# Part of the second layer's sums moved among the tiles of the fourth group, parked in DRAM and added back at the end

## The reference, cut to what matters

```python
h = relu(layernorm(x))
e = leaky_relu((h @ W @ a1)[:, None] + (V @ W @ a2)[None, :])     # V: entity_embs
att = softmax(where(adj > 0, e, -9e15), axis=1)
x1 = x + elu(att @ V + h)
h2 = relu(layernorm(x1))
agg = adj.T @ h2                       # sums over all rows j of adj[j, i] * h2[j]
out = x1 + relu(agg @ U.T / adj.sum(axis=0)[:, None])
```

## Time and profile before

| | |
|---|---|
| median of 3 runs | 389.12 us (388.97 to 389.73) |
| profiled execution, its own time | 388.29 us |
| its span, first to last instruction | 386.5 us |
| mean granted TensorE clock | 0.96 of 2.4 GHz |
| PE busy | 298.7 us (77%), 7586 matmuls |
| DVE busy | 297.3 us (77%) |
| ACT busy | 255.9 us (66%) |
| POOL busy | 114.0 us (29%) |
| HBM read, written | 72.76 MB, 2.11 MB |

### The profile page before, as it was taken

How to read it: one execution, slowest core, us unless ns; L and a number is a source line. 1 busy time by engine, 2 the same in 40 slices (tenths; PEclk the granted TensorE clock), 3 DMA queues, 4 the chain that set the end, 5 groups by cost and what they waited for, 6 DMA issues and landing times.

```text
span 386.5 us, 16271 instructions
## 1 busy us (share of the span) xinstructions
PE 298.7 (77%) x7586; PEld 276.0 (71%) x7586; DVE 297.3 (77%) x403; ACT 255.9 (66%) x316; POOL 114.0 (29%) x120
## 2 busy tenths in 40 slices
PE   1817666556777867578797878778899999999996
PEld 0712555556667756567687877678899999999996
DVE  8899989795998769699985998998988774008333
ACT  2312699689989897779989999996887781010000
POOL 8766287386140482030006111012111103010000
PEclk9956699799989999999999999999999999999999
DMA  8999999999999999995000001001110005102100
GB/s 163 136 109 109 106 109 108 138 109 107 111 123 124 102 109 106 103 104 92 3 4 3 3 4 57 2 3 33 30 30 5 3 5 103 35 2 45 32 22 19
DMA packets 26809, 25.24 MB, mean 65 GB/s; under 512 B 22041, under 2 KB 22105, under 8 KB 26742
## 3 DMA queue, kind: packets, MB, share of 16 engines
q0 software_dynamic: 4752, 16.90, 42.1%
q1 hardware_dynamic: 19830, 6.75, 7.8%
q10 hardware_dynamic: 2160, 0.56, 0.7%
HBM read 72.76 MB, written 2.11 MB: 194 GB/s over the span
## 4 chain that ended last, share of the span: by engine, by line
PE 30%; DVE 29%; ACT 16%; issue 9%; POOL 9%; DMA 6%; SPq 1%; POOLq 0%; DVEq 0%
DVE scratch L832 18%; PE q L1239 10%; PE w L1178 8%; ACT q L686 7%; PE w L1239 6%; DVE arena L884 6%; PE q L1153 5%; ACT arena L668 5%; ACT arena L672 3%; DMA adj_sb<-in_adj_dram 2%; POOL adj_sb L413 2%; DMA v_sb<-n_L_gnn_entity_embs_dram 2%; DMA bi<-rows_sb 2%; POOL stat_c L458 1%; POOL adj_sb L417 1%
## 5 line engine op out<-in xcount | busy, mean ns | idle before, releaser
L1178 PE MATMUL w<-v_sb,arena 128*64 128x65 f32 (+1 forms) x4224 | 155.7, 224 | 9.9 <-issue 8.3
L832 DVE CUSTOM_DVE_ANT_0 scratch<-adj_sb,t_row 125x2048 uint8<-125x2048 uint8 x66 | 153.2, 2322 | 1.6 <-DMA adj_sb<-in_adj_dram 0.3
L1178 PEld LDWEIGHTS w<-v_sb,arena 128*64 128x64 f32 (+1 forms) x4224 | 140.9, 138 | 11.6 <-issue 9.0
L1153 PE MATMUL q<-bi,adj_sb 128*64 128x125 bf16 x2112 | 93.9, 224 | 49.0 <-ACT q L686 41.9
L1153 PEld LDWEIGHTS q<-bi,adj_sb 128*64 128x64 fp8e4 x2112 | 70.4, 112 | 63.4 <-ACT q L686 51.6
L668 ACT ACTIVATE arena<-q,t_col 128x1000 f32<-128x1000 f32 (+2 forms) x102 | 88.5, 872 | 5.9 <-PE q L1153 5.7
L672 ACT ACTIVATE arena<-arena,t 128x1000 f32<-128x1000 f32 (+2 forms) x58 | 63.3, 1093 | 20.6 <-DVE arena L884 19.8
L884 DVE SCALAR_TENSOR_TENSOR arena<-arena,b_col,q 128x1000 f32<-128x1000 f32 (+1 forms) x43 | 52.3, 1224 | 17.4 <-PE q L1153 12.5
L686 ACT ACTIVATE q<-second_row,minus_b 128x750 f32<-128x750 f32 (+1 forms) x49 | 48.1, 981 | 1.3
L686 ACT ACTIVATE q<-arena,minus_b 128x375 f32<-128x375 f32 (+1 forms) x53 | 42.3, 799 | 1.3
L1239 PE MATMUL q<-g_all,adj_sb 124*128 124x129 f16 (+1 forms) x660 | 39.1, 220 | 0.0
(11 more groups left out here) (139 smaller groups left out, 203.6 us busy)
## 6 DMA issues: line engine op xcount, KB each, us to landing
adj_sb<-in_adj_dram POOLq DMA_DIRECT2D x33, 500.0 KB, 36.9
arena<-s_dram SPq DMA_DIRECT2D x2, 500.0 KB, 7.0
out_dram<-v_sb SPq DMA_DIRECT2D x10, 96.0 KB, 1.8
x_sb<-in_x_dram SPq DMA_DIRECT2D x1, 928.0 KB
v_sb<-x_dram SPq DMA_DIRECT2D x1, 768.0 KB, 5.3
v_sb<-n_L_gnn_entity_embs_dram ACTq DMA_DIRECT2D x2, 256.0 KB, 5.4
v_sb<-n_L_gnn_entity_embs_dram SPq DMA_DIRECT2D x2, 256.0 KB, 6.2
second_row<-s_dram SPq DMA_DIRECT2D x1, 500.0 KB, 3.7
```

What stands on the lines that cost most here:

```text
L832: nc.vector.tensor_tensor_reduce(out=junk[0:R, :], in0=adj_bytes[0:R, b, half], in1=t_row[0:R, half], scale=1.0 / ONE, scalar=0.0, op0=ALU ...
L1153: last = nc.tensor.matmul(q[n % Q_SLOTS][e:e + width, bank, start:start + R], weights, bi[:, i % BI_SLOTS, k, :], start=not ON_ACT[n] and ...
L1178: last = nc.tensor.matmul(att(i)[e0:e1, bank, place_in, :], e[:, k * R + e0:k * R + e1], v_sb[:, c, :], start=(c == 0 and place_in == 0), ...
```

## The change

Of the second layer's sums, those over blocks 0 to 8 for outputs 4 to 10 (chunks 12 to 31, 20 of the 32) are made behind tiles of the fourth group, one chunk of nine matmuls at a time, two chunks behind tiles 4, 13 and 28. They are collected in the first bank of `w`, three chunks at a time. ScalarE copies each finished bank into `stage`, which lies in the part of `x_sb` that held x1 of the first blocks, SP writes it to DRAM, and ScalarE's next copy waits until that has landed. At the end of the tile stages SP loads all of it into `t_row`. For outputs 4 to 10 `gather` starts at block 9, and VectorE adds the saved part first. To free `stage`, x1 of the first two groups is stored earlier in SP's queue; to free the bank, `turn_h2` of the third group writes the other one and waits for `s_copied`. The hand-written tables are new throughout. In the core of the diff below the new tables of the groups other than the fourth are cut.

```diff
-                 (1, 4, 6, 8, 10, 12, 28, 29, 30, 31),
-                 (0, 1, 2, 3, 4, 5, 6, 7, 9, 10, 11, ...
+                 (1, 3, 5, 7, 8, 10, 12, 28, 29, 30, 31),
+                 (0, 1, 2, 3, 4, 5, 6, 7, 8, 10, 11, ...
...
-                   (4, 9, 10, 12, 13, 16, 17, 17, 17, 19, 21, 21, 21, 21, 22, 23)]
+                   (4, 10, 13, 13, 13, 13, 16, 17, 17, 18, 20, 20, 21, 23, 23, 24)]
...
-        'elu_below': (None, 6, 7, 6, 8),
+        'elu_below': (None, 7, 7, 5, 8),
-        'scale': (None, 17, 14, 14, 16),
+        'scale': (None, 17, 14, 13, 16),
-        'times_u': (None, 22, 19, 23, 20),
+        'times_u': (None, 21, 19, 25, 21),
-        'copy_s': (15, 7, 18, 12, None),
+        'copy_s': (15, 9, 18, 12, None),
...
+    AHEAD = (4, 5, 6, 7, 8, 9, 10)
+    AHEAD_IN, AHEAD_BLOCKS = 3, 9
+    AHEAD_TILES = (3, 4, 4, 7, 8, 10, 12, 13, 13, 15, 16, 17, 19, 20, 21, 23, 24, 26, 28, 28)
+    AHEAD_COPIES = (5, 10, 13, 17, 22, 26, 30)
+    SAVES = (2, 4, 1)
...
         def turned_at(i):
-            return w[:, i % 2 * 2, :]
+            return w[:, i % 2 * 2 + (i == AHEAD_IN - 1), :]
...
             for i in range(1, NI):
+                if 2 <= i < NI - 1:
+                    sp.wait_ge(mean2_done, i - 1)
+                    store_x1(*GROUPS[i - 2])
+                if i == AHEAD_IN + 1:
+                    save(0, SAVES[0])
                 sp.wait_ge(s_copied, i)
...
+                if i == AHEAD_IN + 1:
+                    save(SAVES[0], SAVES[1])
                 sp.wait_ge(halves_copied, i)
...
-            for i in range(NI - 1):
+            save(SAVES[0] + SAVES[1], SAVES[2])
+            sp.wait_ge(part_saved, 16 * len(AHEAD))
+            sp.wait_ge(r1_ready, NI)
+            sp.dma_start(saved, saved_dram).then_inc(part_loaded, 16)
+            for i in range(2, NI - 1):
...
+            def save(first, n):
+                for k in range(first, first + n):
+                    c0, c1 = OUTS[AHEAD[k]]
+                    sp.wait_ge(part_copied, k + 1)
+                    first = k * 3 * (2 * D + 1)
+                    sp.dma_start(saved_dram[:, first:first + (c1 - c0) * (2 * D + 1)], stage[...]).then_inc(part_saved, 16)
...
+            def copy_ahead(k):
+                c0, c1 = OUTS[AHEAD[k]]
+                act.wait_ge(part_summed, k + 1)
+                if k == 0:
+                    act.wait_ge(x1_stored, 32)
+                    act.wait_ge(cen2_done, 2)
+                else:
+                    act.wait_ge(part_saved, 16 * k)
+                nc.scalar.activation(stage[...], ahead_bank()[...], ACT.Copy).then_inc(part_copied, 1)
...
+                if o in AHEAD:
+                    if o == AHEAD[0]:
+                        dve.wait_ge(part_loaded, 16)
+                    nc.vector.tensor_tensor(saved_sums(o), fresh_sums(o), saved_sums(o), ALU.add).then_inc(part_added, 1)
+                    dve.wait_ge(part_added, AHEAD.index(o) + 1)
...
+                if c == 0 and i == AHEAD_IN + 1:
+                    pe.wait_ge(part_copied, len(AHEAD))
...
+                if i == AHEAD_IN - 1:
+                    pe.wait_ge(s_copied, i + 2)
...
+            def sum_ahead(k, c):
+                c0, c1 = OUTS[AHEAD[k]]
+                if c == c0:
+                    if k == 0:
+                        pe.wait_ge(hp_done, AHEAD_IN)
+                        pe.wait_ge(lo_done, AHEAD_IN - 1)
+                        pe.wait_ge(ones_made, 1)
+                    else:
+                        pe.wait_ge(part_copied, k)
+                for b in range(AHEAD_BLOCKS):
+                    rows = rows_of(b)
+                    last = nc.tensor.matmul(ahead_bank()[:, ...], adj_sb[0:rows, b, c * P:(c + 1) * P], h2[0:rows, b, 0:2 * D + 1],
+                                            start=(b == 0 and c == c0), stop=(b == AHEAD_BLOCKS - 1 and c == c1 - 1))
+                if c == c1 - 1:
+                    last.then_inc(part_summed, 1)
...
+                if i == AHEAD_IN:
+                    for tile, chunk in zip(AHEAD_TILES, chunks_ahead):
+                        if tile == c:
+                            sum_ahead(*chunk)
...
             for o in (0, 1, 2, 3):
-                gather(o, 0, late)
+                gather(o, blocks_ahead(o), late)
             turn_h2(NI - 1)
-            gather(4, 0, late)
+            gather(4, blocks_ahead(4), late)
             times_u(NI - 1)
-            gather(5, 0, late)
+            gather(5, blocks_ahead(5), late)
...
-                gather(o, 0, NB)
+                gather(o, blocks_ahead(o), NB)
```

More of the change, by code:

```diff
@@ L180, in graph_layers_kernel @@
         junk = scratch[:, 0:512].bitcast(uint8)
+        saved = t_row[:, 0:sum(OUTS[o][1] - OUTS[o][0] for o in AHEAD) * (2 * D + 1)]
+        stage = x_sb[:, :, :].rearrange("p b d -> p (b d)")[:, 0:3 * (2 * D + 1)]
+        saved_dram = nc.dram_tensor("saved_dram", (P, sum(OUTS[o][1] - OUTS[o][0] for o in AHEAD) * (2 * D + 1)), fp32, kind="Internal").ap()
         s_dram = nc.dram_tensor("s_dram", (NI, 8 * R), fp32, kind="Internal").ap()
@@ L337, in out_bank, with ahead_bank, fresh_sums, saved_sums @@
             return banks[(0, 1, 2, 3, 4, 5, 6, 7)[o % 8]]
+        def ahead_bank():
+            return w[:, (AHEAD_IN - 1) % 2 * 2, :]
+        def fresh_sums(o):
+            c0, c1 = OUTS[o]
+            return out_bank(o)[:, 0:(c1 - c0) * (2 * D + 1)]
         def sums(o):
+            return (saved_sums(o) if o in AHEAD else fresh_sums(o)).rearrange("p (k d) -> p k d", d=2 * D + 1)
+        def saved_sums(o):
             c0, c1 = OUTS[o]
-            return out_bank(o)[:, 0:(c1 - c0) * (2 * D + 1)].rearrange("p (k d) -> p k d", d=2 * D + 1)
+            first = AHEAD.index(o) * 3 * (2 * D + 1)
+            return saved[:, first:first + (c1 - c0) * (2 * D + 1)]
+        def blocks_ahead(o):
+            return AHEAD_BLOCKS if o in AHEAD else 0
         @block.sync
@@ L355, in _, with store_x1 @@
                 sp.dma_start(u_sb[:, h * D:(h + 1) * D], U[:, :]).then_inc(u_in, 16)
+            def save(first, n):
[3 more added lines that the diff above has]
+                    first = k * 3 * (2 * D + 1)
+                    sp.dma_start(saved_dram[:, first:first + (c1 - c0) * (2 * D + 1)], stage[:, 0:(c1 - c0) * (2 * D + 1)]).then_inc(part_saved, 16)
+            def store_x1(b0, b1):
+                rows = rows_of(b0)
+                to = x1_dram[first_row(b0):first_row(b0) + (b1 - b0) * rows, :].rearrange("(k p) d -> p k d", p=rows)
+                sp.dma_start(to, x_sb[0:rows, b0:b1, :]).then_inc(x1_stored, 16)
             for i in range(1, NI):
@@ L718, in _ @@
                         copy_halves(i + 1)
+                if i == AHEAD_IN:
+                    for k, tile in enumerate(AHEAD_COPIES):
+                        if tile == c:
+                            copy_ahead(k)
                 if n + 2 < len(TILES) and ON_ACT[n + 2]:
@@ L1206, in times_u @@
                 last.then_inc(h2_multiplied, 1)
+            chunks_ahead = [(k, c) for k, o in enumerate(AHEAD) for c in range(*OUTS[o])]
+            def sum_ahead(k, c):
[9 more added lines that the diff above has]
+                    rows = rows_of(b)
+                    last = nc.tensor.matmul(ahead_bank()[:, (c - c0) * (2 * D + 1):(c - c0 + 1) * (2 * D + 1)],
+                                            adj_sb[0:rows, b, c * P:(c + 1) * P], h2[0:rows, b, 0:2 * D + 1],
+                                            start=(b == 0 and c == c0), stop=(b == AHEAD_BLOCKS - 1 and c == c1 - 1))
+                if c == c1 - 1:
+                    last.then_inc(part_summed, 1)
             rows()
@@ L1240, in gather @@
                                                 adj_sb[0:rows, b, c * P:(c + 1) * P], h2[0:rows, b, 0:2 * D + 1],
-                                                start=(b == 0 and c == c0), stop=(b == NB - 1 and c == c1 - 1))
+                                                start=(b == blocks_ahead(o) and c == c0), stop=(b == NB - 1 and c == c1 - 1))
                 if last_one == NB:
```

54 lines of the change are left out of this document (27 added, 27 removed), and 10 rows, old and new, of tables (DVE_TILES, GUARD_TILES).

## The result

The changed kernel takes 413.09 us (median of 4 runs, 412.55 to 414.33) against 389.29 us; the ratio is 1.0615, with a 95% interval of 1.0587 to 1.0643. It was forecast at 380.3 us and is 23.8 us slower instead of 8.8 faster. The profiled execution took 413.43 us, with a span of 411.6. Runs over 1.5% above the fastest of the same kernel are left out as slow, which in this document concerns only two of the six of `after_split`.

What follows compares the result with a forecast made beforehand. The prediction took TensorE to bound the end and VectorE to close the fourth group. Its terms, -10.5 + 0.4 + 1.3 = -8.8 us, took the median of 389.12 to 380.3 us, own range 379.2 to 382.3, wider range 378.6 to 384.8.

Steps and rivals of the forecast that it cites:

- the price of group 0's early store: SP's queue ahead of the third group: 12.8 us pass, row still in time, costed at nothing, at most some 8 us.
- Rival 2: Early x1 store holds the third group's row, which starts 7 us late: up to 387.5 us, half of that 384; chance 0.13.
- The end, -10.5 + 0.4: At the end, 180 matmuls removed save 10.5 us; only VectorE's last addition is on the path, costing 0.4 us.
- the cover: Output 5's early part, 48 matmuls or 2.8 us, still covers the last group's closing by 0.2 us; costed at nothing.
- The fourth group, +1.3: VectorE ends the fourth group later: 0.5 us at tile 12, 2.33 more for a guard, 1.5 less for a wait.
- rival 4: In the fourth group, ScalarE's copies wait for saves to land; kernel would take 395 us, slower; chance 0.04.
- rival 3: TensorE becomes the fourth group's bound, half of the 10.5 us landing on the path: 384.3 us; chance 0.10.
- The tables, 0 with 1 us to both sides: The other groups' new tables move steps by a tile or two, no direction seen: 0, 1 us either way.
- Rival 5: Change doesn't do what it says: gain void if the wait for the saved part held VectorE at output 4; chance 0.01.

Runs made afterwards that it cites:

- after_split: Changed kernel with each early x1 store cut in two, rows 0 to 111 and then 112 to 123; 379.83 us, ratio 0.978 to the kernel before.
- late_x1: Changed kernel with x1 of groups 0 and 1 stored behind the adjacency load, in SP's fourth round; 379.01 us, ratio 0.9733 to the kernel before.
- act_queue_group0: Changed kernel with group 0's early x1 store issued from ScalarE's queue instead of SP's, group 1's staying on SP; 377.90 us, one run.

## Why the prediction was wrong

The sign was wrong by one step: the price of group 0's early store. I wrote "Group 0's x1 is 372 rows of 256 bytes, 23 for an engine" and from it 12.8 us, a row that lands at 133 for a need at 134.28, and a cost of nothing. The price of a row, one adjacency packet of 0.55 us, was right (0.57 measured). So was the mechanism, a row that waits behind the store in SP's queue. The number of rows an engine was not: 93, not 23, as the store goes over four engines. With 93 the same sum gives 109.81 + 93 x 0.55 + 10.6 = 171.6 for the row's landing; ScalarE's relu came at 171.51. I took the sixteen engines for granted; no row shown before the run said how a store of 124 rows is spread, and I should have bounded it.

The Trainium skill has the rule (DMA: Bandwidth & Descriptors, section Why a DMA increments its semaphore by 16 and not by 1, on how many engines): a transfer goes over the largest number of engines up to 16 that divides the slowest dimension on both sides. By it 124 rows get four engines and 112 get sixteen, and the runs agree: 23.2 us for 124 rows, 18.4 for 336, with 4 and 16 packets left over. The profile doesn't number the engines, so which four they were is not shown.

Rival 2 named the place and the mechanism and had 0.13. Its price, 21 us for the store and up to 387.5, stopped short by the same error. Its lean on the arbitration of the Trainium skill (DMA: Bandwidth & Descriptors, section Queues, rings and completion order: a whole packet of 9 to 17 descriptors from one queue before the next) is not borne out here, as the profile counts packets: single rows alternate with single packets of 4 KB, 0.63 us apart. Its 0.9 us a packet was too high as well; rival 2 had the price of a row too large and the number of rows too small.

The other terms:
- **The end, -10.5 + 0.4.** Measured -10.1 (66.7 to 56.6), in every kernel with these 20 chunks ahead. In late_x1 the early part of outputs 4 and 5 and the work around it are:
```profile
338.22 2.96 PE L1335 MATMUL w<-g_all,adj_sb 124*128 124x129 f16 x48
341.02 1.09 PE L1277 MATMUL w<-uu,buf_b 128*125 128x128 f32 x8
341.94 2.96 PE L1335 MATMUL w<-g_all,adj_sb 124*128 124x129 f16 x48
344.75 5.76 PE L1335 MATMUL q<-g_all,adj_sb 124*128 124x129 f16 x96
```
  48 matmuls are 2.81 us from start to start, 58.5 ns each. POOL ends the low part at 343.40 + 1.12 = 344.52, and TensorE goes on at 344.75: the cover holds by the 0.2 us of the forecast:
```profile
343.40 1.12 POOL L569 TENSOR_TENSOR g_all<-buf_a,g_all 125x512 f16<-125x512 f32 x1 [13.51 <-ACT buf_a L709]
```
  The last addition is one of 0.43 us:
```profile
372.99 0.43 DVE L1085 TENSOR_TENSOR t_row<-q,t_row 128x258 f32<-128x258 f32 x1 [0.40 <-PE q L1335]
```
  The 81 ns a pair of the Trainium skill (TensorE: Matmul & The Clock Gate, section Back-to-back issue gap) would have taken 14.6 us from the end; the traces show 58.4 to 58.5 ns and 10.1 us, so here the measurement decides.
- **The fourth group, +1.3.** From its first mask to that of the fifth I had forecast 64.6 us; in the kernel after it is 236.80 to 301.19, 64.4. VectorE's last shift instruction came 59.5 us after the first mask, forecast 59.7. The lines of the kernel after, PE first:
```profile
236.80 0.65 PE L1220 MATMUL q<-bi,adj_sb 128*64 128x125 bf16 x16 [1.31 <-DMA bi<-rows_sb]
...
301.19 0.67 PE L1220 MATMUL q<-bi,adj_sb 128*64 128x125 bf16 x16
```
```profile
296.31 0.17 DVE L938 TENSOR_TENSOR halves<-neg_t,halves 125x8 bf16<-125x8 f32 x1
```
  The growth came with the new tables, in which the forecast had put it (the order of the guards), and not with the sums: with the new tables alone the same distance is 64.7 us, against 63.3 before. ScalarE's copies took 0.48 us (forecast 0.45), and the saves landed in 1.9 us, so rival 4 is out. TensorE's waits for ScalarE's relu in late_x1 fell to 1.6 us from the 12.2 of the earlier trace rows: the sums went where the idle time was. VectorE's scores waited 5.6 us for TensorE there, against 5.3 before, so rival 3 is out as well.
- **The tables, 0 with 1 us to both sides.** Measured -2 us (387.12 against 389.18), outside what I gave them. Without the early store the terms would have summed to -10.1 + 0.8 + 0.3 for the sums and -2 for the tables, -11.0; late_x1 shows -10.2. The 0.8 between them is mostly the third group's 0.6, whose cause stays open. What the tables won lies ahead of the fourth group: with them alone its first mask starts at 202.06 us instead of 203.87. That would account for the 1.3 us by which late_x1 lies under the forecast of 380.3.
- **Rival 5.** SP loads the saved part back behind the fifth group's shifts, not at the end of the tile stages: in the kernel after at 304.15, landed in 6.8 us, for a first addition at 387.93. Nothing waited for it.

## What to carry to other kernels

A store that is moved forward has two prices: what it moves, and who stands behind it in its queue. Count the latter in rows of the engine that gets most, not in rows over 16: a transfer whose outer dimension is 124 used four engines here (a dimension of 125 would get five by the rule above, which no run tested), and beside the bulk load each of its rows waited for a bulk packet. Put it behind what is urgent, on another queue, or cut it so that the outer dimension of the large part is a multiple of 16. Each of the three brought 33 us or more here (late_x1, act_queue_group0, after_split).

## What the runs showed of the hardware that I had not expected

- 124 rows went slower through a busy queue than 336 did (23.2 against 18.4 us), because 336 were 112 x 3.
- Rows of 256 and of 768 bytes cost the same there (23.2 and 23.4 us for 124).
- An issue on SP behind the store can block SP itself: `s_dram<-rows_sb` took 13.2 and 14.7 us to issue behind 372 rows, against 0.34 to 0.37 behind 124 or 336, and 0.27 in after_split, 2 us behind 372 rows in two parts. What it waited for in there the profile doesn't say.
- SP's queue isn't held by a store in ScalarE's: from there the same 372 rows cost the kernel nothing (377.9 us, one run), though they passed at the same 7.1 packets a us.
- With 124 rows only four series of packets run, each with one row between two packets of 0.625 us of the bulk load.
